# Cross-attention phase of a decoder layer: whole projections in one slot, value matmuls in groups of eight tiles, sixteen probability tiles

## The reference, cut to what matters

```python
def _L0_xattn_ref(x, c, Wq, bq, Wk, bk, Wv, bv, Wo, bo):   # x, c: (16, 256, 512), 16 heads of 16 channels
    q = jnp.einsum('oc,bct->bot', Wq, x) + bq[None, :, None]
    k = jnp.einsum('oc,bct->bot', Wk, c) + bk[None, :, None]
    v = jnp.einsum('oc,bct->bot', Wv, c) + bv[None, :, None]
    ...
    scores = jnp.einsum('bhkt,bhks->bhts', q, k) * SCALE
    p = jax.nn.softmax(scores, axis=-1)
    out = jnp.einsum('bhts,bhks->bhkt', p, v)
    ...
    return jnp.einsum('oc,bct->bot', Wo, out) + bo[None, :, None]
x = _layernorm(x + _L0_xattn_ref(x, ctx_2048, ...), axis=-1)
```

## Time and profile before

| | us |
|---|---|
| median of three runs | 2120.29 |
| lowest and highest run | 2104.89, 2120.82 |
| the profiled execution | 2100.74 |
| its span, first to last instruction | 2098.9 |
| busy: PE, DVE, ACT, POOL | 1948.0, 1513.9, 1133.2, 997.0 |

### The profile page before, as it was taken

One profiled execution on the slowest core, in us unless ns is written; L12 is line 12 of the kernel. 1 busy time (PEld: TensorE's weight loads), 2 busy tenths in 40 slices (PEclk: granted clock), 3 DMA queues, 4 the chain that ended last, 5 costly groups with the idle time before them and its releaser, 6 DMA issues.

```text
span 2098.9 us, 31715 instructions
## 1 busy us (share of the span) xinstructions
PE 1948.0 (93%) x11390; PEld 1045.0 (50%) x11424; DVE 1513.9 (72%) x2635; ACT 1133.2 (54%) x2117; POOL 997.0 (47%) x980
## 2 busy tenths in 40 slices
PE   3799999899999888999999999999999898999997
PEld 1667777677767643344434444444444333444443
DVE  4246585566656656777878888887888728999997
ACT  3144444344434433677878877887888673333331
POOL 6345455455554531444444444443444326666664
PEclk9899999999999877999999999999999989999999
DMA  4678786777778653556776655556665510111111
GB/s 138 114 132 138 157 144 130 144 135 161 148 124 150 117 98 52 87 89 127 133 123 112 109 106 107 107 108 103 113 101 105 152 53 11 51 41 41 41 61 41
DMA packets 149515, 220.55 MB, mean 105 GB/s; under 512 B 41463, under 2 KB 50167, under 8 KB 148615
## 3 DMA queue, kind: packets, MB, share of 16 engines
q1 hardware_dynamic: 139886, 217.74, 53.7%
q10 hardware_dynamic: 9472, 0.79, 0.4%
HBM read 83.95 MB, written 32.02 MB: 55 GB/s over the span
## 4 chain that ended last, share of the span: by engine, by line
PE 52%; DMA 19%; DVE 12%; POOL 6%; ACT 3%; issue 3%; SPq 3%; ACTq 0%; POOLq 0%; DVEq 0%
PE bank L1565 7%; PE bank L1236 7%; PE bank L1271 7%; PE bank L85 6%; DMA xa_sums<-xa_oc 5%; PE bank L1541 4%; PE bank L86 4%; PE bank L87 4%; PE bank L1279 4%; DMA sa_kst<-sa_part_kl 4%; DMA inv<-xa_sums 4%; PE bank L506 3%; DMA xa_den<-inv 2%; PE bank L531 2%; DVE sa_mneg L574 2%
## 5 line engine op out<-in xcount | busy, mean ns | idle before, releaser
L1314 DVE TENSOR_REDUCE xa_mneg<-bank 128x1 f32<-128x512 f32 x1024 | 657.8, 681 | 193.7 <-PE bank L1279 190.1
L1136 ACT ACTIVATE xa_prob<-bank 128x512 f32<-128x512 f32 x1024 | 568.9, 600 | 204.9 <-PE bank L1271 195.7
L1279 PE MATMUL bank<-xa_kst,xa_qst 48*128 48x512 f32 x1024 | 411.3, 475 | 23.1 <-DVE xa_mneg L1314 14.9
L1271 PE MATMUL bank<-xa_qst,xa_kst 49*128 49x512 f32 x1024 | 398.4, 460 | 14.3 <-ACT xa_prob L1136 13.9
L402 ACT ACTIVATE sa_prob<-bank 128x512 f32<-128x512 f32 x256 | 152.4, 598 | 370.3 <-PE bank L531 369.7
L1271 PEld LDWEIGHTS bank<-xa_qst,xa_kst 49*128 49x128 f32 x1024 | 161.7, 189 | 329.5 <-ACT xa_prob L1136 257.6
L1236 PE MATMUL bank<-xa_prob,xa_v 128*32 128x512 f32 x2048 | 283.8, 627 | 0.0
L1473 POOL TENSOR_TENSOR ff_total<-ff_prod,ff_mag 128x512 f32<-128x512 bf16 x128 | 194.5, 1520 | 108.6 <-DVE ff_mag L1589 108.6
L574 DVE TENSOR_REDUCE sa_mneg<-bank 128x2 f32<-128x512 f32 x256 | 164.2, 682 | 51.6 <-PE bank L543 51.3
L1279 PEld LDWEIGHTS bank<-xa_kst,xa_qst 48*128 48x128 f32 x1024 | 164.0, 190 | 58.5 <-DVE xa_mneg L1314 38.4
L1517 ACT ACTIVATE ff_gelu<-bank 128x512 bf16<-128x512 f32 x128 | 75.5, 592 | 160.9 <-PE bank L1565 158.7
(11 more groups left out here) (185 smaller groups left out, 3730.6 us busy)
## 6 DMA issues: line engine op xcount, KB each, us to landing
xa_qst<-xa_part_q SPq DMA_DIRECT2D x192, 128.0 KB, 5.4
xa_kst<-xa_part_k SPq DMA_DIRECT2D x192, 128.0 KB, 6.8
sa_qst<-sa_part_qh SPq DMA_DIRECT2D x64, 256.0 KB, 6.2
sa_kst<-sa_part_kh SPq DMA_DIRECT2D x64, 256.0 KB, 9.0
xa_den<-inv SPq DMA_DIRECT2D x64, 256.0 KB
sa_xraw<-xT SPq DMA_DIRECT2D x8, 1024.0 KB, 8.5
sa_qst<-sa_part_ql SPq DMA_DIRECT2D x32, 256.0 KB, 6.0
sa_kst<-sa_part_kl SPq DMA_DIRECT2D x32, 256.0 KB, 10.3
```

The source lines that it names most:

```text
L1136: act.activation(prob[:, e % XPROBS, :], banks[eb[e]][:, :], ACT.Exp, scale=X_SCALE)\
L1271: pe.matmul(banks[eb[e]][:, :], kst[u % 3][rows_of, head // 2, t * P:(t + 1) * P], qst[u % 3][rows_of, head // 2, :], start=True, stop=Tru ...
L1279: pe.matmul(banks[mb[m]][:, :], qst[u % 3][rows_of, n // 8, t * P:(t + 1) * P], kst[u % 3][rows_of, n // 8, :], start=True, stop=True).the ...
L1314: dve.tensor_reduce(mneg[:, u % 2, column:column + 1], banks[mb[m]][:, :], AX.X, ALU.max, negate=True).then_inc(s_mfree, 1)
```

## The change

It does five things. A projection is issued whole, at one slot: q at slot 2, k at 10, o at 18 and v at 26 of a unit, so every eighth slot has one. Value matmuls are issued for eight tiles at once, every eight slots, four slots away from the projections. There are 16 places for probabilities (each a tile of its own now, four of them in the region "output", used from the third unit on). The exp tiles and what hangs on them begin two slots later, and the steps of the denominators are drawn together: the multiplication on POOL stands 17 slots behind the copy (before 21), the addition 35 (39), oh 37 (41), ol 39 (43). The turn of the maxima, at slot 10, stands beside the whole k projection. The feed-forward part has some tiles at other addresses and the last of its first steps two slots later.

```diff
-XPROBS = 12
+XPROBS = 12, 16
...
-    MAX_AT, TURN_AT, EXP_AT = S + 8, 2 * S + 10, 2 * S + 18
+    MAX_AT, TURN_AT, EXP_AT = S + 8, 2 * S + 10, 2 * S + 20
     BATCH = 2 * S
+    GROUP = 8
+    VALUES_AT = EXP_AT + GROUP + 2
     OUT_AT = EXP_AT + 19
...
     for u in range(U):
-        part_slots["q", u] = [S * u + 2, S * u + 6]
-        part_slots["k", u] = [S * u + 10, S * u + 14]
+        slot_of["q", u] = S * u + 2
+        slot_of["k", u] = S * u + 10
     for b in range(NB):
-        part_slots["v", b, 0] = [BATCH * b + 26, BATCH * b + 30]
-        part_slots["v", b, 1] = [BATCH * b + 50, BATCH * b + 54]
-        part_slots["o", b, 0] = [BATCH * (b + 2) + 58, BATCH * (b + 2) + 62]
-        part_slots["o", b, 1] = [BATCH * (b + 3) + 18, BATCH * (b + 3) + 22]
+        for t in range(CC):
+            slot_of["v", b, t] = BATCH * b + S * t + 26
+            slot_of["o", b, t] = BATCH * (b + 2) + S * t + 50
     for t in range(CC):
-        part_slots["o", NB - 1, t] = [BATCH * (NB + 1) + n for n in ((26, 58), (60, 62))[t]]
+        slot_of["o", NB - 1, t] = BATCH * (NB + 1) + (58, 60)[t]
...
+    place, prob_before = in_turn(S * U, *(range(n) for n in XPROBS), S * 2)
...
-            if (un := output_half(slot, 9)):
+            if (un := output_half(slot, 7)):
...
-            if (un := output_half(slot, 14)):
+            if (un := output_half(slot, 11)):
...
-            if (un := output_half(slot, 21)):
+            if (un := output_half(slot, 17)):
...
-                wait.wait_ge(s_av, (e - XPROBS) // 4 + 1)
-                left.values(wait)
-                act.activation(prob[:, e % XPROBS, :], banks[eb[e]][:, :], ACT.Exp, scale=X_SCALE)\
+                if prob_before[e] is not None:
+                    wait.wait_ge(s_av, prob_before[e] // GROUP + 1)
+                elif place[e] < XPROBS[0]:
+                    left.values(wait)
+                else:
+                    left.output(wait)
+                act.activation(prob[place[e]][:, :], banks[eb[e]][:, :], ACT.Exp, scale=X_SCALE)\
                    .then_inc(s_exp, 1)
...
-            if (un := unit(slot, OUT_AT + 41, 1)):
+            if (un := unit(slot, OUT_AT + 37, 1)):
...
-        def values(u, quad):
-            half, t = quad // 4, quad % 4
-            wait.wait_ge(s_exp, S * u + 4 * quad + 4)
+        def values(u, group):
+
+            half, t0 = group // 2, group % 2 * 2
+            wait.wait_ge(s_exp, S * u + GROUP * (group + 1))
...
-            for j in range(4):
-                last = pe.matmul(ob[32 * j:32 * j + 32, :],
-                                 v[(u // 2) % 2][:, t, half, 4 * (u % 2) + j, :],
-                                 prob[:, (S * u + 4 * quad + j) % XPROBS, :],
-                                 start=(t == 0), stop=(t == TT - 1))
+            for t in (t0, t0 + 1):
+                for j in range(4):
+                    last = pe.matmul(ob[32 * j:32 * j + 32, :],
+                                     v[(u // 2) % 2][:, t, half, 4 * (u % 2) + j, :],
+                                     prob[place[S * u + 16 * half + 4 * t + j]][:, :],
+                                     start=(t == 0), stop=(t == TT - 1))
...
-            if (un := unit(slot, EXP_AT + 34, 1)):
-                values(un[0], 7)
-            if (un := unit(slot, EXP_AT + 6, S - 7)) and un[1] % 4 == 0:
-                values(un[0], un[1] // 4)
+            if (un := unit(slot, VALUES_AT)) and un[1] % GROUP == 0:
+                values(un[0], un[1] // GROUP)
...
-            for job, i in parts_in.get(slot, []):
-                project_part(job, i)
+            for job in jobs_in.get(slot, []):
+                for i in range(2):
+                    project_part(job, i)
...
-FFN_AT = [1022, 1046, 1070, 1078, 1086, 1094, 1106]
+FFN_AT = [1022, 1046, 1070, 1078, 1086, 1094, 1108]
```

68 lines of the change are left out of this document (34 added, 34 removed).

## The result

The changed kernel takes 2156.06 us in the median of its runs (2144.0 to 2159.66), the kernel before beside it 2116.74: a ratio of 1.0185, 95% interval 1.0125 to 1.0245. The interval leaves out 1, so it is slower, by 39 us. The forecast was 2155. The profiled execution took 2144.0 us.

The account below looks back on a forecast made before the run. TensorE (PE) was taken to bound cross-attention. Eight slots: 6.95 us clean plus 0.31 waits, 7.26 against 6.94, so +35 us over 876 slots: 2136 us, 2155 on the median's scale; 8-in-10 range 2110 to 2200.

Parts of the forecast that it names:

- burst of four pairs: TensorE, four exp and max matmul pairs in a row: held by three banks per side, 1.75 us instead of 1.14.
- clean round: Eight cross-attention slots on TensorE without further waits: 1.75 + 1.60 + 1.75 + 1.85 = 6.95 us, against 6.45 before.
- chain, per 64 slots: Three VectorE instructions ending an output projection, 1.6 us: next burst ends 0.4 late, twice per batch, 0.8 us (before 1.2).
- turns, per 64 slots: Turn of the maxima becomes a fifth tile in a burst, waiting 0.2 us for a bank, twice per batch: 0.4 us.
- row of maxima: First exp tile of a unit waits for this row by DMA; starting two slots later covers such gaps: 0, at most 0.5.
- key stacks: Max matmuls wait for the DMA stacks of the keys: kept at 1.0 us per batch.
- denominators: Reciprocal on VectorE may wait for the sums' DMA, now 4.1 us later instead of 6.0: 0.3 us per batch, ends 0 and 3.4.
- join: Feed-forward part's new tile addresses and start moved by two slots: 0 us, bounds -3 and +5.
- the switches win: Rival, bursts before each block: banks return early, bursts under 1.59 us, 2012 us fully free, 2066 at half; chance 0.10.
- No difference: Rival: bursts cost 0.5 us, but bank waits swallow the others; eight slots 7.07 us, +14 us, 2134 us; chance 0.27.
- The round trip of the denominators: Third rival: VectorE stands at the reciprocal, ScalarE at oh, each unit; +43 us, 2198; chance 0.16 including the clock.
- The clock: Possibility, counted with the third rival: TensorE's clock falls to the 1.2 GHz level oftener; joint chance 0.16, above 2180 us.

Follow-up runs that it names:

- The two runs with half the columns: Changed kernel with maxima over 256 of 512 columns, then also exponents of 256 columns from the fourth unit on: 2139.46 and 2107.03 us, one execution each.
- the exchange with the later steps: Changed kernel with second-half v at slot 50 and first o at 58, multiplication, addition, oh and ol at 19, 38, 41, 43 behind the copy: 2149.12 us.

## Why the prediction was right, and where it was not

**The sum.** Per 64 slots it said 8 x 6.95 + 2.5 = 58.1 us, and 57.99 were measured. By its own steps:

| term | predicted | measured |
|---|---|---|
| burst of four pairs | 1.75 | 1.74 |
| value block of eight | 1.85 | 1.86 |
| projection, whole | 1.60 | 1.58 (what is left of 6.92) |
| clean round | 6.95 | 6.92 |
| chain, per 64 slots | 0.8 | 0.84 (7.35 and 7.33) |
| turns, per 64 slots | 0.4 | 0.44 (7.11 and 7.17) |
| row of maxima | 0 | 0 |
| key stacks | 1.0 | near 0 |
| denominators | 0.3 | 1.2 to 1.3 |
| start of the phase | 0 | within the 12 us by which executions differ |
| join | 0 | 14.9, of which 12.0 behind the last maximum |

**The mechanism** was the burst, and it was found because the kernel before already had two such bursts near the end of the phase. The rows of after repeat them: fourth exp at 1.18, next block at 1.74. The two runs with half the columns show that it is the banks, by taking the readers' time and nothing else: they gave back 0.27 of the 0.60 us by which a burst exceeds its matmuls.

**The rule of the skill.** The value block and the projection save what the changes of block between them cost, about 0.18 us each: the blocks take 3.44 us per eight slots after, and took 3.78 before. The Trainium skill, TensorEngine Tiling (Array Packing), section Key Properties, says that a change of tiling mode drains TensorE; the trace agrees. The round of 5.73 us that the rule alone would give is not reached, since longer blocks between fewer changes want longer bursts, and the burst costs 0.6 us more than its matmuls.

**The denominators** were sized too small: 0.3 against 1.2 per 64 slots, which the exchange with the later steps priced. The prediction looked at the wrong door. It expected the reciprocal on VectorE to wait, and weighed its distance from the sums' DMA, 4.1 against 6.0 us; that wait fell to 1.2 us in all, which fits the argument on the query stacks and doesn't show it. The time was lost further on, where the distance from the copy to `xa_oh` had been cut by four slots and the trips to DRAM and back (7.00 and 4.18 us here, 7.60 and 3.56 in the earlier trace rows) had not become shorter. The row for it was in the earlier trace rows, 3.9 us. And the gap of the earlier trace rows, which the prediction put down to the row of maxima, was ScalarE behind `xa_oh` and the rounding of x, the same place.

**The key stacks** cost nearly nothing and had been carried over at 1.0; why they fell isn't shown. That error and the last one cancel to 0.1 per 64 slots, which is luck.

**The join** was put at nothing, with bounds of -3 and +5, "because PE is not full in that join". It measured +14.9 between the two profiled executions. At most 2.9 of it is the longer stall for the sums. The other 12.0 lie behind the last maximum, where bursts of four exp tiles and blocks of eight value tiles alternate too: TensorE stands for ScalarE 5.7 us more, and is busy 6.2 us more at a lower granted clock. Idle time on the bounding engine had been taken for slack, when it was waiting that the change lengthens.

**How much was luck.** The two profiled executions differ by 43 us where the sum said 35. At 0.04 us per slot it has 31 for the 768 slots of the stretch, which took 29.5 more; what it lacks is the join. The forecast added 20 us for the scale of the medians, and the changed kernel's median lies only 12 above its profile. The median of 2156 against 2155 is closer than the steps deserve; the difference of the medians, 39, against 35 is the fair comparison.

**The rivals.** That the switches win needed a burst under 1.59 us, and it took 1.74. No difference needed most of the bank waits to fall into time lost anyway; every clean round shows them. The round trip of the denominators was real, at about a third of its price, and on ScalarE. The clock, which the third rival took in, was 1.00 in the stretch and counted only in the join.
